# One product for the split maxima of four heads, and key rows that say whose maximum is whose

## The reference

```python
H, Hd = 16, 16
q = (query @ Wq.T + bq).reshape(B, Sq, H, Hd).transpose(0, 2, 1, 3)      # query: layernorm(x), Sq = 112
k = (key @ Wk.T + bk).reshape(B, Skv, H, Hd).transpose(0, 2, 1, 3)        # key, value: the context, Skv = 375
v = (value @ Wv.T + bv).reshape(B, Skv, H, Hd).transpose(0, 2, 1, 3)
q = q * SCALE
scores = jnp.einsum('bhqd,bhkd->bhqk', q, k)
attn = jax.nn.softmax(scores, axis=-1)
out = jnp.einsum('bhqk,bhkd->bhqd', attn, v)
out = out.transpose(0, 2, 1, 3).reshape(B, Sq, D)
return out @ Wo.T + bo
```

## Time and profile before

| what | value |
|---|---|
| runs, median (lowest to highest) | 612.32 us (611.78 to 615.21) |
| the profiled execution's own time | 611.59 us |
| its span | 609.9 us |
| PE busy | 432.1 us, 71%, 3489 matmuls |
| DVE busy | 424.7 us, 70%, 1712 instructions |
| ACT busy | 274.2 us, 45% |
| POOL busy | 78.2 us, 13%, 227 instructions |
| maxima, L2087 | 128 matmuls of 112 columns, median 212 ns |
| copy of the maxima, L1242 | 32 instructions, 630 ns |
| `ks<-onesb` | 3 DMAs of 35.2 KB |

### The profile page before, as it was taken

How to read it: one execution, slowest core, us unless ns; L and a number is a source line. 1 busy time by engine, 2 the same in 40 slices (tenths; PEclk the granted TensorE clock), 3 DMA queues, 4 the chain that set the end, 5 groups by cost and what they waited for, 6 DMA issues and landing times.

```text
span 609.9 us, 10358 instructions
## 1 busy us (share of the span) xinstructions
PE 432.1 (71%) x3489; PEld 298.6 (49%) x3489; DVE 424.7 (70%) x1712; ACT 274.2 (45%) x657; POOL 78.2 (13%) x227
## 2 busy tenths in 40 slices
PE   3798799722293994756899999999999665504305
PEld 3467685511162652724577777676455553103302
DVE  7545999899938687758788888865444665374574
ACT  3754544822223543435365656664533452352340
POOL 6780000000066000034700000000000000000000
PEclk9997799755578897769699999999999888856557
DMA  9700004195025980000575948700300361000002
GB/s 277 199 2 1 1 2 151 54 205 121 2 61 122 134 146 26 1 0 4 148 129 72 212 73 148 187 2 1 138 1 1 129 217 70 0 1 2 0 1 60
DMA packets 34666, 47.23 MB, mean 77 GB/s; under 512 B 5542, under 2 KB 32055, under 8 KB 32823
## 3 DMA queue, kind: packets, MB, share of 16 engines
q1 hardware_dynamic: 34614, 46.58, 32.4%
HBM read 37.87 MB, written 8.60 MB: 76 GB/s over the span
## 4 chain that ended last, share of the span: by engine, by line
PE 57%; DVE 23%; ACT 11%; issue 5%; POOL 2%; DMA 1%; DVEq 0%; ACTq 0%; POOLq 0%
PE ps L2116 7%; PE ps L2070 4%; DVE PR L1029 4%; PE ps L2057 4%; ACT below L1719 4%; PE ps L2046 4%; PE ps L1861 4%; PE ps L1973 3%; PE ps L1869 3%; PE ps L2032 3%; PE ps L2242 2%; PE ps L1925 2%; DVE prod L1025 2%; DVE below L1349 2%; PE ps L1820 2%
## 5 line engine op out<-in xcount | busy, mean ns | idle before, releaser
L1221 DVE TENSOR_REDUCE negm<-ps 112x1 f32<-112x375 f32 x128 | 66.0, 544 | 11.0 <-PE ps L2046 7.8
L1690 ACT ACTIVATE E<-ps 125x448 f32<-125x448 f32 x96 | 52.2, 544 | 46.7 <-PE ps L2057 46.5
L2215 PE MATMUL ps<-cnt,same 128*128 128x3 bf16 (+4 forms) x40 | 6.9, 174 | 61.5 <-ACT below L1719 41.1
L2046 PE MATMUL ps<-ks,qs 96*112 96x375 bf16 x128 | 44.0, 355 | 2.9 <-ACT qs L1683 2.5
L2070 PE MATMUL ps<-E,v 125*32 125x112 f32 x768 | 42.7, 273 | 0.0
L2057 PE MATMUL ps<-qs,ks 99*125 99x112 bf16 x384 | 40.6, 230 | 1.2 <-DVE qs L1242 0.7
L2057 PEld LDWEIGHTS ps<-qs,ks 99*125 99x125 bf16 x384 | 35.4, 142 | 9.8 <-issue 6.3
L1209 DVE TENSOR_REDUCE acts<-gel 128x4 f32<-128x448 f32 x32 | 19.8, 620 | 29.3 <-ACT gel L1658 29.3
L2215 PEld LDWEIGHTS ps<-cnt,same 128*128 128x128 bf16 (+1 forms) x40 | 4.5, 112 | 65.0 <-issue 65.0
L1658 ACT ACTIVATE gel<-ps 128x448 f32<-128x448 f32 x32 | 17.3, 544 | 29.3 <-PE ps L2116 29.3
L1242 DVE CAST qs<-ps 3x448 bf16<-3x448 f32 x32 | 20.2, 630 | 12.3 <-PE ps L2087 12.2
(11 more groups left out here) (374 smaller groups left out, 1110.8 us busy)
## 6 DMA issues: line engine op xcount, KB each, us to landing
ks<-key_parts SPq DMA_DIRECT2D x48, 187.5 KB, 6.6
piw<-fn_process_input_weights SPq DMA_DIRECT2D x8, 1024.0 KB, 4.8
key_parts<-kp SPq DMA_DIRECT2D x48, 93.8 KB
ctx_again<-in_ctx SPq DMA_DIRECT2D x7, 512.0 KB
keys<-kx SPq DMA_DIRECT2D x16, 187.5 KB, 2.1
kx<-keys SPq DMA_DIRECT2D x8, 375.0 KB, 6.2
ctxP<-in_ctx SPq DMA_DIRECT2D x8, 256.0 KB, 6.4
patn<-in_L_ffn_input_patterns SPq DMA_DIRECT2D x1, 2048.0 KB, 16.5
```

Source lines behind the costliest of these rows:

```text
L1221: drain(dve.tensor_reduce(negm[:, n:n + 1], bank(nm)[0:S, 0:SC], AX.X, ALU.max, negate=True), nm)
L1690: drain(fn(E[:, (KCH * f + c) % 6, :], bank(nm)[0:KC, 0:4 * S], ACT.Exp), nm)
L2046: fill(mm(bank(nm)[0:S, 0:SC], qs[0:SR, u // 4 % 3, n, :], ks[0:SR, u // 4 % 3, n, :], start=True, stop=True), nm)
```

## The change

`MR` = 12 rows take the place of three. One product of `maxima` now turns the 112 by 12 block of `negp` (four heads by three parts) into 12 rows of 112 columns. VectorE's copy reads these 112 columns for each of the four heads and writes them four times side by side into rows 96 to 107 of `qs`: each head has the maxima of all four below its queries. Which of them count is said by `ks`: for the i-th head of a group, rows 96 + 3i to 98 + 3i are ones and the other nine zeros. GpSimd makes that pattern in a new tile `kones` (12 x 4 x 375) with a MEMSET and two selects, after its wait for the path and ahead of the split of the keys, and three DMAs write it into `ks`, four times each; they wait for the new semaphore `kones_ready`. The score products contract over 108 rows.

```diff
--- before.py
+++ after.py
@@ -28,6 +28,7 @@
 Q_PARTS = (0, 0, 1, 1, 2, 0)
 SR = HD * len(K_PARTS)
 LAG = 5
+MR = 4 * 3
 UP0 = 3
 ACT_ROUNDS = (1, 3, 5)
 
@@ -338,6 +339,7 @@
         rd = Region(max(rx.at, rn0.at, r_at + 4 * B * CT * S))
         turn = [rd.take(f"turn{d}", [128, 128]) for d in range(2)]
         meet = [rd.take(f"meet{d}", [128, KB, 128]) for d in range(2)]
+        kones = Region(rd.at - 2 * 4 * KB * 128).take("kones", [MR, 4, SC], BF16)
         scratch = Region(rw.at + 4 * CT * B * D)
         lanes_at = scratch.take("lanes_at", [128, 2, 2, 32], BF16)
         zerob = scratch.take("zerob", [128, 2], BF16)
@@ -508,6 +510,7 @@
              "k_split pv_part cnt_ready tie_ready sel_ready gel_ready gel_used acts_ready "
              "pmx_ready pmd_ready pexp_ready vec scl pol").split()]
 
+        kones_ready = sem("kones_ready")
         parts_stored = [sem(f"parts_stored{i}") for i in range(2)]
         keys_stored = [sem(f"keys_stored{i}") for i in range(4)]
         keys_loaded = [sem(f"keys_loaded{i}") for i in range(2)]
@@ -627,8 +630,10 @@
                 load_keys(b + 2)
             sp.wait_ge(x_ready, B)
             sp.wait_ge(consts_ready, 1)
+            sp.wait_ge(kones_ready, 1)
             for b in range(3):
-                sp.dma_start(ks[SR:SR + 3, b, :, :], onesb[0:3, :].unsqueeze(1).broadcast_to([3, NH, SC])
+                sp.dma_start(ks[SR:SR + MR, b, :, :].rearrange("p (g i) s -> p g (i s)", i=4),
+                             kones[:, :, :].rearrange("p i s -> p (i s)").unsqueeze(1).broadcast_to([MR, NH // 4, 4 * SC])
                              ).then_inc(loaded["ones_k"], 16)
             for b in range(2):
                 load_stack(b)
@@ -775,6 +780,13 @@
                 pool.tensor_tensor(part[:, :, 2, :], x32, part[:, :, 1, :], ALU.subtract).then_inc(k_split, 1)
 
             wait_drained(pool, ("path", 0))
+            did(pool.memset(kones[:, :, :], 1.0))
+            settle()
+            did(pool.affine_select(out=kones[:, :, :], in_=kones[:, :, :], compare_op=ALU.is_ge, fill=0.0, base=0,
+                                   pattern=[[-3, 4], [0, SC]], channel_multiplier=1))
+            settle()
+            pool.affine_select(out=kones[:, :, :], in_=kones[:, :, :], compare_op=ALU.is_ge, fill=0.0, base=2,
+                               pattern=[[3, 4], [0, SC]], channel_multiplier=-1).then_inc(kones_ready, 1)
             for b in range(4):
                 split_keys(b)
             wait_drained(pool, "bo")
@@ -1239,8 +1251,8 @@
                         nm = ("negT", f + 1)
                         wait_filled(dve, nm)
                         n = 4 * ((f + 1) % 4)
-                        drain(dve.tensor_copy(qs[SR:SR + 3, (f + 1) // 4 % 3, n:n + 4, :].rearrange("p n s -> p (n s)"),
-                                              bank(nm)[SR:SR + 3, 0:4 * S]), nm)
+                        drain(dve.tensor_copy(qs[SR:SR + MR, (f + 1) // 4 % 3, n:n + 4, :],
+                                              bank(nm)[SR:SR + MR, 0:S].unsqueeze(1).broadcast_to([MR, 4, S])), nm)
                 if t == 0 and 1 <= b <= B - 1:
                     statistics(3, b - 1)
                     if b == HB:
@@ -2055,7 +2067,7 @@
                 for i in range(4):
                     n = 4 * (f % 4) + i
                     ins = mm(bank(nm)[0:KC, S * i:S * i + S],
-                             ks[0:SR + 3, f // 4 % 3, n, KC * c:KC * c + KC], qs[0:SR + 3, f // 4 % 3, n, :],
+                             ks[0:SR + MR, f // 4 % 3, n, KC * c:KC * c + KC], qs[0:SR + MR, f // 4 % 3, n, :],
                              start=True, stop=True)
                 fill(ins, nm)
 
@@ -2083,10 +2095,9 @@
                 nm = ("negT", f)
                 claim(pe, nm)
                 pe.wait_ge(neg_ready, f // 4 + 1)
-                for i in range(4):
-                    ins = mm(bank(nm)[SR:SR + 3, S * i:S * i + S], negp[:, f // 4 % 2, 4 * (f % 4) + i, :],
-                             identb[0:S, 0:S], start=True, stop=True)
-                fill(ins, nm)
+                n = 4 * (f % 4)
+                fill(mm(bank(nm)[SR:SR + MR, 0:S], negp[:, f // 4 % 2, n:n + 4, :].rearrange("p n c -> p (n c)"),
+                        identb[0:S, 0:S], start=True, stop=True), nm)
 
             def token_transposes(h, half):
 
```

## The result

The changed kernel takes **615.78 us** (median of 20 runs, 611.21 to 618.38). The kernel before, run beside it, takes 613.02 (20 runs, 611.15 to 618.32). The ratio is 1.0042, 95% interval 1.0025 to 1.0058: slower by about 2.6 us. That lies inside the 0.5% I had called "the same", but 615.78 is above the top of my range, 615.0. The profiled execution took 615.94 us for a span of 612.5, against 609.9 for the span before.

A forecast was written before the change was run, and what follows sets the result against it. TensorE was taken to bound the attention loop, VectorE held by GpSimd the stretch before. 611.59 - 4.3 + 4.0 = 611.3 us for the profiled execution, 612.0 us with 0.7 to the median; range 607.5 to 615.0.

The forecast's parts named there:

- the same: Whole kernel: within 0.5% of the kernel before, neither under 609.3 nor over 615.4 us; chance 0.60.
- Minus 4.3 us in the loop: Attention loop, TensorE: one maxima product for four saves 0.14 us a pass over 31 passes; bounds 3.4 to 5.0.
- rival 2: Attention loop: a removed product is worth more than 0.05 us; at 81 ns 7.5 us won, 608.8 us; chance 0.06.
- Copy, 108 rows: Attention loop: VectorE's copy of the maxima stays 0.63 us, and 108 contraction rows for 99 cost nothing; both zero.
- The price of the GpSimd work: GpSimd ahead of the key split: MEMSET and two selects take 4.9 us, between 4.7 and 5.7.
- The ones for the keys (SP's queue): SP's DMAs: larger DMAs of ones move the queue back some 5 us, under cover of over 40 us; zero.
- Plus 4.0 us for the shift: Before attention: the key split, 4.9 us later, holds VectorE's SBUF-only instructions and delays TensorE's restart by 4.0 us.
- my spread: Cost of the moved key split: shifts of 4.7 to 5.3 us give 3.8 to 4.4, 5.5 to 5.7 give 2.9 to 3.1.
- rival 1: Key split: the shift costs little, 0.6 us, for instance if held instructions fall into gaps; 608.6 us; chance 0.22.
- The removal of products as nothing but a gain: Attention loop, TensorE: fewer maxima products counted only as a saving, 4.3 us, with no term for loading the program.
- A wait of TensorE for keys or ones: Attention queries: sign of a wrong forecast, TensorE waiting for late stacks or ones; that would take over 40 us of delay.

The follow-up runs named there:

- the load moved: Changed kernel with the 1 MB load of the `oiwn` weights one stack of keys later: 608.94 us, ratio 0.9922; measured again 611.77 us, ratio 0.9971.
- the ones in the FFN: Changed kernel, three GpSimd instructions behind the second SiLU, DMAs of ones further back: 614.47 us, ratio 1.0032; with the `oiwn` load one stack later 610.13 us, 0.9957.
- the padding: Empty TensorE instructions ahead of the first FFN products: 120 in the changed kernel, 611.19 us, ratio 0.9970; 136 in the kernel before, 614.90 us, ratio 1.0040.
- four products on twelve rows: Changed kernel with its one maxima product issued four times over, on the same 12 rows: 613.75 us, ratio 1.0007.
- the shift alone: Kernel before with only the three new GpSimd instructions ahead of the split, their tile used by nobody: 615.05 us, ratio 1.0028.
- twice the shift: Changed kernel, `oiwn` load one stack later, three GpSimd instructions done twice ahead of the split: 605.87 us, ratio 0.9877; again 606.72 us, ratio 0.9905.
- the ones behind the split: Changed kernel with its three GpSimd instructions behind the split of the keys, DMAs of the ones behind the first two stacks: 619.44 us, ratio 1.0061.

## Why the prediction was wrong

*Minus 4.3 us in the loop: right.* 4.2 in the two profiles with the load moved (140.36 - 136.14 and 136.16), 3.7 and 3.4 with the ones in the FFN and with the padding (136.65, 136.92), and four products on twelve rows take it away again. A removed product was worth 0.05 us in this chain, as the starts said, so rival 2 is out: three products at 81 ns, the figure of the Trainium skill, TensorE: Matmul & The Clock Gate, Back-to-back issue gap, would have given 7.5.

*Copy, 108 rows: right.* Both zero: four products on twelve rows take as long as the old four.

*The price of the GpSimd work: nearly right.* 4.38 us from the MEMSET to the first CAST, under my 4.7 to 5.7; I took 4.9.

*The ones for the keys (SP's queue): right.* Zero: TensorE waited for no ones or stack, and its first queries are 110.38 us behind the expansion, against 110.19.

*Plus 4.0 us for the shift: mis-sized.* The mechanism is as described, though I put it too widely: the trace has VectorE instructions on SBUF alone that aren't held, such as the RECIPROCAL of L1049, 0.18 us at 189.97 beside the TENSOR_TENSOR of 189.95. One profile, that of the shift alone, gave 3.8. But I held the arrival of the fourth block's keys fixed relative to the split. It was not: the rows show 1.02 us of idle GpSimd after the change, and there the held instructions flow. In the six profiles with this shift the restart moved by 0.4, 0.4, 0.5, 1.7, 1.9 and 3.8 us, so the top of my spread is what I took for its middle; rival 1, "the held instructions fall into gaps", was nearer to this part of it. In the changed kernel it was 0.5. With twice the shift the sign turns (-2.5 and -3.3).

*The removal of products as nothing but a gain: here is the step that failed.* The sum has no term for what fewer instructions do to the loading of TensorE's program; I put it at nothing without a reason. I asked what the removed instructions took on TensorE, and not that they are part of a program which comes in over the same DMA engines as the data. With 6 instructions less a pass, the packet that this place needed came at the end of the burst of 358 to 371 us. The stand and the half clock behind it cost 5.15 us in the profiled execution, more than the loop gained. "A wait of TensorE for keys or ones" was my sign of being wrong; it came as a wait of TensorE for nothing that the profile names. That the median still came out only 0.8 us above my range is luck: in the profiled execution the shift cost 3.5 us less than I took, and hid most of the 5.15 that I had left out.

The sum by the profiles: -4.2 in the loop and +5.15 for stand and half clock make +0.9 in the loop's stretch. The stretch from the expansion to the first queries adds 0.2 (of the 0.5 at the restart 0.3 is made good by then), and what lies ahead of the expansion another 0.2. The two executions are 4.35 us apart. Of the rest, 1.3 lie behind the first pattern product (189.65 us to the end against 188.35). The last 1.75 lie outside the span and belong to this one execution: 3.4 us lie around its span, and 1.7 to 2.0 around those of the other 19. I have no cause for either. Between the medians, 2.8 us apart, about 1.5 is left over.

**What stays open.** Profiles are one execution each: how often the key load comes late, and how often the clock falls after a stand, isn't known (in the changed kernel and with the ones behind the split it fell, in the two others with a stand it did not, and in none of the ten without). The 20 runs of the changed kernel lie in two groups, 8 from 611.21 to 614.41 us and 12 from 615.52 to 618.38; whether that is the clock behind the stand isn't shown either. The kernel with the ones in the FFN and the load moved has the loop's gain without the shift, and its median gained 2.7 us, not 4.2. That the packets of "q8 instruction" are TensorE's rests on the padding and on their timing against the stands; the profile doesn't name an engine.

## What to carry to other kernels

Where TensorE stands on "issue" between two instructions of one group while the DMA engines are full, look at the instruction queue in the DMA view: try the neighbouring load one step later, and a few instructions that do nothing, before blaming the change at hand. When instructions are removed from a long unrolled program, the later parts of it are loaded at other times against the transfers (here 359 us became 369), so the gain has to be read in its own stretch (here 140.4 to 136.1 us) as well as in the total. And when GpSimd work is shifted beside VectorE's work on SBUF, replay it with the loads that it waits for shifted too.

## What the runs showed of the hardware

- TensorE's program comes over the DMA engines in packets of 0.02 MB (136 or 120 empty instructions bring one more, at 189 us) and can be late behind data: stands of 1.4 to 1.9 us, made by 136 empty instructions, and removed by 120 or by moving one load.
- A stand of TensorE can be followed by half the granted clock: from about 374 to 380.5 us behind the stand of 1.89, 3.3 us lost. It did so behind 1.89 and 1.64, not behind 1.61 and 1.38.
- A TENSOR_SCALAR of VectorE with four elements in each partition ends with the GpSimd instruction beside it: L1059 0.97 and L1062 0.75 us in the changed kernel, 0.17 and 0.14 for the same two in the first profile of the kernel with the GpSimd work done twice, where GpSimd stood idle. The RECIPROCAL between them isn't held: 0.18 us in both.
- On GpSimd a MEMSET of 12x1500 took 1.34 us and an AFFINE_SELECT of the same 1.46 to 1.48, 0.98 ns an element.
